# Moving the later query and key products of an attention kernel past the row-maxima chain on Trainium2

## The reference, cut to what matters

```python
h = _layernorm(x, axis=-1) * (1 + ca) + sa
qkv = h @ W_qkv.T + b_qkv
qkv = qkv.reshape(b, t, 3, N_HEADS, D_HEAD)
...
scores = jnp.einsum('bhqd,bhkd->bhqk', Q, K) / np.sqrt(D_HEAD)
attn = jax.nn.softmax(scores + causal, axis=-1)
O = jnp.einsum('bhqk,bhkd->bhqd', attn, V)
...
return O @ W_o.T + b_o
```

## Time and profile before

| what | value |
|---|---|
| median of 3 runs | 990.87 us (990.5 to 992.32) |
| span of the profiled execution, first to last instruction | 985.5 us |
| PE busy | 890.2 us, 90% |
| DVE busy | 712.9 us, 72% |
| ACT busy | 580.1 us, 59% |
| POOL busy | 350.7 us, 36% |
| mean granted TensorE clock | 0.975 |

### The profile page before, as it was taken

How to read it: one execution, slowest core, us unless ns; L and a number is a source line. 1 busy time by engine, 2 the same in 40 slices (tenths; PEclk the granted TensorE clock), 3 DMA queues, 4 the chain that set the end, 5 groups by cost and what they waited for, 6 DMA issues and landing times.

```text
span 985.5 us, 19308 instructions
## 1 busy us (share of the span) xinstructions
PE 890.2 (90%) x6090; PEld 529.1 (54%) x6164; DVE 712.9 (72%) x2285; ACT 580.1 (59%) x1268; POOL 350.7 (36%) x311
## 2 busy tenths in 40 slices
PE   7899899998899999989999987888899999999990
PEld 4443335433535434544443453432798899999880
DVE  7898776879566889657689668899547575444588
ACT  3335676766676777586676757757535433333563
POOL 4200030530430324323023444024585465565530
PEclk8998999999999999999999999999999999999996
DMA  6484535525506336253464565105332323222699
GB/s 204 122 176 108 79 110 111 91 72 98 79 1 144 68 79 144 76 70 95 73 123 105 127 114 180 36 26 177 110 97 76 96 73 105 73 81 75 194 313 306
DMA packets 83235, 110.61 MB, mean 112 GB/s; under 512 B 15930, under 2 KB 56434, under 8 KB 83138
## 3 DMA queue, kind: packets, MB, share of 16 engines
q1 hardware_dynamic: 75234, 88.40, 38.2%
q0 software_dynamic: 6816, 18.62, 6.0%
q10 hardware_dynamic: 1088, 2.36, 0.6%
HBM read 69.42 MB, written 35.41 MB: 106 GB/s over the span
## 4 chain that ended last, share of the span: by engine, by line
PE 64%; DVE 17%; ACT 9%; issue 6%; POOL 3%; DMA 1%; another core or an unknown queue 1%; SPq 0%; ACTq 0%; DVEq 0%; POOLq 0%
PE PY L1608 10%; PE PO L1741 9%; PE PH L1608 9%; PE PM L1698 9%; PE PS L1721 8%; ACT PR L1073 3%; PE PHT L1826 3%; DVE MXF L1410 3%; DVE JK L1407 3%; PE PX L1753 2%; PE PX L1662 2%; PE PS L1725 2%; PE PX L1673 1%; PE PX L1770 1%; POOL SF L912 1%
## 5 line engine op out<-in xcount | busy, mean ns | idle before, releaser
L1073 ACT ACTIVATE PR<-PS 128x512 f32<-128x512 f32 (+3 forms) x768 | 335.3, 499 | 125.6 <-PE PS L1725 85.6
L1407 DVE CUSTOM_DVE_ANT_0 JK<-PM,MK 128x128 bf16<-128x128 f32 (+3 forms) x512 | 239.5, 485 | 54.9 <-PE PM L1698 52.5
L1698 PE MATMUL PM<-QK 128*128 128x512 bf16 (+3 forms) x725 | 234.3, 332 | 22.9 <-DVE MXF L1410 11.6
L1721 PE MATMUL PS<-QK 128*128 128x512 bf16 (+3 forms) x737 | 235.0, 330 | 11.7 <-ACT PR L1073 9.2
L1410 DVE TENSOR_REDUCE MXF<-PM 128x1 f32<-128x512 f32 x256 | 175.2, 684 | 76.8 <-PE PM L1698 61.0
L1721 PEld LDWEIGHTS PS<-QK 128*128 128x128 bf16 x768 | 75.5, 99 | 167.2 <-ACT PR L1073 105.3
L1741 PE MATMUL PO<-PR,V 128*17 128x512 f32 (+3 forms) x1536 | 162.3, 495 | 0.2 <-DVE MXA L1407 0.2
L1698 PEld LDWEIGHTS PM<-QK 128*128 128x128 bf16 x768 | 75.5, 98 | 94.7 <-DVE MXF L1410 33.6
L1608 PE MATMUL PY<-W2S,HT 128*128 x852 | 119.4, 289 | 2.6 <-issue 1.8
L1725 PE MATMUL PS<-MT,identb 128*128 128x128 bf16 x512 | 111.4, 220 | 1.6 <-issue 0.8
L1608 PE MATMUL PH<-W1S,XT 128*128 x426 | 111.7, 397 | 0.6 <-DVE W2S L1562 0.6
(11 more groups left out here) (282 smaller groups left out, 1159.2 us busy)
## 6 DMA issues: line engine op xcount, KB each, us to landing
QK<-SD SPq DMA_DIRECT2D x180, 128.0 KB
SD<-SP SPq DMA_DIRECT2D x42, 256.0 KB, 2.9
OP<-OS SPq DMA_DIRECT2D x64, 64.0 KB
LP<-LR SPq DMA_DIRECT2D x64, 64.0 KB
W1S<-in_w SPq DMA_DIRECT2D x8, 512.0 KB, 6.6
X<-XA SPq DMA_DIRECT2D x3, 1024.0 KB, 8.4
H2D<-XA SPq DMA_DIRECT2D x3, 1024.0 KB, 4.8
YG<-YT SPq DMA_DIRECT2D x12, 256.0 KB
```

Of the source, the lines that this page charges most:

```text
L1073: eng.activation(PR[:, slot, i, c0:512], PS[m % 3][:, c0:512], ACT.Exp, scale=0.25).then_inc(S["exp"].sem, 1)
L1407: eng.tensor_tensor_reduce(JK[:, jk % 2, 0:w], PM[m % 3][:, 0:w], MK[:, 512 - w:512], 1.0, -3.0e38, ALU.add, ALU.max, MXA[:, mb, h, qt:qt ...
L1698: eng.matmul(PM[m % 3][:, 0:128 * (k1 - k0)], QK[:, r, h, 0, qt * 128:(qt + 1) * 128], QK[:, r, h, 1, k0 * 128:k1 * 128], start=True, stop ...
L1721: last = eng.matmul(PS[m % 3][:, c0:512], QK[:, r, h, 1, j * 128:(j + 1) * 128], QK[:, r, h, 0, 512 * f + c0:512 * f + 512], start=True, s ...
```

## The change

One table of steps replaces the formula, for units 2 to 7, and the store is hung one step later. Even units keep their first two products at steps 9 and 11; odd units get them at 9 and 11 instead of 11 and 13. The third and the fourth go for all six units to 18.5 and 20.5, behind `crow`. The store's place is step 24, which is step 0 of the next stretch.

```diff
+QK_AT = (9, 11, 18.5, 20.5)
...
-            place(*((0, NEXT_QK[n]) if u == 1 else (2 * u - 3, (9, 11)[u % 2] + 2 * n)), [(0, ("qk", u, which, half)), (1, ("qk_hi", u, which, half)), (2, ("qk_lo", u, which, half))])
+            place(*((0, NEXT_QK[n]) if u == 1 else (2 * u - 3, QK_AT[n])), [(0, ("qk", u, which, half)), (1, ("qk_hi", u, which, half)), (2, ("qk_lo", u, which, half))])
         if u:
-            place(*((0, SD1_AT) if u == 1 else (2 * u - 3, 23)), one("sd", u, 2))
+            place(*((0, SD1_AT) if u == 1 else (2 * u - 3, 24)), one("sd", u, 2))
...
-LATE = ()
...
-    "bvb": {"bvb": 2},
+    "bvb": {"bvo": 2},
...
-                        eng.tensor_copy(BVB[:, c, :], BV[:, c:c + 1].broadcast_to([128, 128])).then_inc(S["bvb"].sem, 1)
+                        eng.tensor_copy(BVB[:, c, :], BV[:, c:c + 1].broadcast_to([128, 128])).then_inc(S["bvo"].sem, 1)
```

More of the change, by code:

```diff
@@ L394 @@
     "gat": {f"yg{i}": (lambda n, i=i: 32 * (gat_ring(n) == i)) for i in range(RING + NT)},
-    "comb": {"cmb_a": 1, "comb": 2, "cmb_d": lambda n: int(n not in LATE), "cmb_p": lambda n: int(n in LATE)},
+    "comb": {"cmb_a": 1, "comb": 2, "cmb_d": 1},
     "out_st": {f"o{i}": (lambda n, i=i: 16 * (gat_ring(n) == i)) for i in range(RING + NT)},
@@ L855, in sync_program @@
                     n = a[0]
-                    sp.wait_ge(*after("cmb_p" if n in LATE else "cmb_d", "comb", n))
+                    sp.wait_ge(*after("cmb_d", "comb", n))
                     eng.dma_start(out[n // NT, 128 * (n % NT):128 * (n % NT) + 128, :], XR[gat_ring(n)][:, :]
@@ L864, in gpsimd_program @@
             const = S["const"].sem
-            done = {n: 0 for n in ("const", "sub_p", "neg_p", "gbo", "div_p", "om", "bias", "h2", "both", "cmb_p")}
+            done = {n: 0 for n in ("const", "sub_p", "neg_p", "gbo", "div_p", "om", "bias", "h2", "both")}
             newest = []
@@ L993, in gpsimd_program @@
                         bounds_check=EMPTY - 1 + B * T * 2, oob_is_err=True).then_inc(S[f"ys{t % 4}"].sem, 16)
-                elif kind == "comb" and a[0] in LATE:
-                    n = a[0]
-                    r = gat_ring(n)
-                    po.wait_ge(*after("comb", "comb", n))
-                    turn("cmb_p")
-                    eng.tensor_tensor(XR[r][:, :], YG[r][:, 0, :], XR[r][:, :], ALU.add).then_inc(S["cmb_p"].sem, 1)
         def scalar_program(eng):
@@ L1591, in vector_program @@
                     eng.tensor_tensor(YG[r][:, 0, :], YG[r][:, 0, :], GB[:, n // NT, :], ALU.mult).then_inc(sem, 1)
-                    if n not in LATE:
-                        dv.wait_ge(S["comb"], c + 2)
-                        eng.tensor_tensor(XR[r][:, :], YG[r][:, 0, :], XR[r][:, :], ALU.add).then_inc(S["cmb_d"].sem, 1)
+                    dv.wait_ge(S["comb"], c + 2)
+                    eng.tensor_tensor(XR[r][:, :], YG[r][:, 0, :], XR[r][:, :], ALU.add).then_inc(S["cmb_d"].sem, 1)
         def tensor_program(eng):
@@ L1707, in tensor_program @@
                 elif kind == "bvo":
-                    pe.wait_ge(*after("bvb", "bvb"))
+                    pe.wait_ge(*after("bvo", "bvb"))
                     px_free(pe, step)
```

## The result

The changed kernel takes 1014.61 us, the median of four runs (1011.73 to 1018.11), against 990.68 us before: a ratio of 1.0245 with a 95% interval of 1.0217 to 1.0272, 24 us slower. The forecast was 996.7 us, between 988 and 1001.5. The direction was right, the size a quarter of what came.

What follows compares the result with a forecast made beforehand. PE, 90% busy, was taken to bound the kernel, with DVE bounding stretch 4 until the `out` products. Terms -4.0 + 0.9 + 8.9 = +5.8 us on 990.9 gave 996.7 us, range 988 to 1001.5.

Steps and rivals of the forecast that it cites:

- Cost 8.9 us: Late copies in SP's queue make DVE's reciprocal wait; PE loses 4.0, 1.9 and 3.0 us in stretches 4, 8, 12.
- The gain, -4.0: PE's waits at `crow` go, 2.6 us in odd units 3, 5, 7, and gaps in stretches 1, 5, 9, 1.4 us.
- the new waits, +0.9: The third product now waits for DVE's copy out of PX behind `crow`: 0.15 us for each of six units.
- Stretch 4's chain from the new place to the copies, 7.5 us: Copies start 7.5 us after PE reaches the fourth product's new place: 4.3 us later for group 6, 3.5 for 10 and 14.
- The copies don't absorb this: SP's time from first copy to `lsum` does not shrink, so `lsum` is later by the whole shift.
- The wait ahead of the reciprocal: DVE idles ahead of the reciprocal for about 4, 2 and 5 us in stretches 4, 8 and 12.
- small in 2, 6, 10: DVE's wait for the reciprocal's input in these stretches: 0.4 us each, costing PE nothing.
- ACT's and DVE's parts: The moved products' work on ACT and DVE costs the same at its new place, so nothing was added.
- if PE catches up: Sign of a wrong size: PE recovers behind the stall, so DVE's idle time does not lengthen the stretch.
- all delays paid in full: Rival: no cushion in stretch 12 and slow `lsum` transfers everywhere, cost 14.5 us, 1002.3 us in all; chance 0.10.
- The faster rival: Copies get shorter by what they start later, so no cost and -3.1 us: 987.8 us; chance 0.15.
- The distance of 5.4 us between span and median: Profiled span 985.5 us against the runs' median of 990.9; the prediction kept this distance for the changed kernel.

Runs made afterwards that it cites:

- g_recip: The changed kernel with DVE's reciprocal of the row sums two steps later: 1000.51 us, ratio 1.0114 to the kernel before.
- n_pool: The kernel before with three more POOL subtractions in each of stretches 4, 8 and 12, no added DVE work: 996.26 us, ratio 1.0081.
- m_delay_recip: The kernel before with SP's copies of even groups held until a score of the running stretch, and the reciprocal two steps later: 996.93 us, ratio 1.0109.
- c_fill2: The changed kernel plus unread products on PE, 22 in stretch 4 and 16 each in 8 and 12: 1005.87 us, ratio 1.0167 to the kernel before.
- b_delay: The kernel before, only with SP waiting for a score of the running stretch before the copies of even groups: 1009.67 us, ratio 1.0211.
- a_all_early: The changed kernel with every unit's four products at steps 9, 11, 13, 15 and the store at 23: 987.79 us, ratio 0.9971; run again, 988.25 us.
- d_fourth: The changed kernel with the products at steps 9, 11, 13 and 18.5 and the store at 24: 1000.18 us, ratio 1.0104 to the kernel before.

## Why the prediction was right in direction and wrong in size

- **The step that failed is "Cost 8.9 us".** It was added up from the stalls behind the reciprocal alone, 4.0, 1.9 and 3.0 us in stretches 4, 8 and 12, and these came: 4.6, 2.3 and 2.45, 9.4 together. But the three stretches are 26.8 us longer. The sum had nothing for two terms, the half clock, 11.9 us by the estimate from the windows and most of it right behind stalls, and PE's waits at the start of stretches 8 and 12, 5.5 us.
- **The gain, -4.0, and the new waits, +0.9: right in sum, by luck.** The waits named are gone, and the six odd stretches came out 3.3 us shorter for 3.1, 0.5 of it the clock in stretch 1. But stretches 3, 7 and 11 were to be 1 us shorter each and are -1.0, +0.3 and +0.2, while 1, 5 and 9 gave 2.7 us for a forecast of 1. In 7 and 11 PE has new waits for PM, of 0.49 and 0.60 us, that the sum did not have; their cause is open.
- **Stretch 4's chain from the new place to the copies, 7.5 us: right**, copies 4.1 us later for 4.3. **For stretches 8 and 12 too short by 2.8 us**: copies 6.35 us later for 3.5. Some 1 us of it is the place: I took it from the earlier trace rows, 370.73, 4 us before stretch 7 ends, and the fourth product's copy in fact starts 2.57 us before the end in 7 and 11, as in 3. The other 1.9 us is DVE: the third product's cast took 1.41 us, and the fourth's started only at 382.46, behind DVE's own work in the new stretch, 3.5 us into it where it was 1.1 in stretch 4.
- **"The copies don't absorb this": right, and they got longer**, by 1.2 to 1.8 us from first copy to `lsum`.
- **The wait ahead of the reciprocal came near, partly by luck**: forecast 4, 2 and 5 us, measured 4.71, 3.57 and 5.10. `lsum` is 8.1 and 7.8 us later in stretches 8 and 12 where I had 3.5, but DVE itself comes to the reciprocal 3.2 and 3.5 us later, and the two errors offset each other; "small in 2, 6, 10": 1.43, 0 and 0.74. Those three stretches, forecast at nothing, cost 2.9 us, of which 0.6 us each is there without any wait too (stretch 6, and all three in g_recip).
- **"ACT's and DVE's parts" of the moved products cost nothing: wrong.** I used the exclusion between POOL and DVE for the length of the chain and did not charge it to DVE, which has no room at the start of stretches 8 and 12: 2.8 us each. n_pool shows that POOL's subtractions there cost time by themselves, and m_delay_recip that stretch 8 has its old length without the late work; how the 2.8 us divide between DVE's added cast and POOL's subtractions is not shown.
- **The larger missing term is the clock behind the stalls**, 11.9 us by the estimate from the windows; c_fill2 got 8.7 us back, net of its added work, in part by shorter waits. The sum took a microsecond of PE's idle time as a microsecond. My sentence that I would be wrong in size "if PE catches up" looked at the wrong side.
- **The rival "all delays paid in full"** had somewhat nearer waits (4.3 and 2.8 us in stretches 4 and 8) and, for the same reason, the wrong price. **The faster rival**, copies that get shorter, fell: they got longer. **The queue itself was right**: b_delay brings 19 of the 24 us without moving a product, and moving the reciprocal alone gave back 14.
- The distance of 5.4 us between span and median was one execution's luck; 1.7 to 1.9 is what lies around a span. It changes nothing in the forecast, which is the median and 5.8 us.

What stays open: why the clock falls where it does in stretches 12 to 14. The falls come and go between the executions of one kernel (a_all_early's profiled execution took 998.6 us with them, its median is 987.8), so a share of the clock read from one trace is a rough one. And why d_fourth takes 1000.2 us with hardly a wait of the reciprocal.

## What to carry to other kernels

Price a stall of TensorE twice: its length, and the half-clock time behind it, which here was more than the stalls of the reciprocal, 11.9 us for 9.4. When moving work to an engine that looks idle, ask which other engine shares something with it in that very place. And follow a moved step down the queue that carries its result: what stands behind the late store decided this kernel. Another queue freed it, but the engine that owns that queue had to stand and wait, and it was one on which PE depends.

## What the runs showed of the hardware that was not expected

- The clock fell once behind gaps of PE of 0.16, 0.42 and 0.53 us, the only ones over 0.1 us from 556 to 568 us, in stretch 12 ahead of the reciprocal's wait. The trace before has gaps of 0.42 and 0.53 us at the same place and the clock stays at 1.00. What made the difference is not shown. Windows of the changed kernel, before the fall and in it:

```profile
562.00:568.00 6.00, 4.89 (x37) 2.39 (x40) 3.80 (x14) 5.87 (x15) 5.53 (x5) 1.00 1.09 127
568.30:571.70 3.40, 3.40 (x15) 1.88 (x12) 1.45 (x9) 2.55 (x5) 3.04 (x3) 0.51 1.11 231
```

- Useless products can pay: 54 of them took 8.7 us off a kernel with stalls, and put 8.7 us on one without (g_recip).
- A TENSOR_SCALAR with one input of eight columns took 1.00 us beside a subtraction on POOL, in place of 0.15.
- Which of two starts first decides who pays: a cast on DVE 0.03 us behind POOL's subtraction took 1.41 us, one 0.12 us ahead of it took 0.42, and then POOL's subtraction took 1.31 in place of 1.15.
- Small transfers on ACT's queue ran beside 12 large copies on SP's and were through 6 us before them; on SP's own queue they started when the copies were nearly done.
